# A window-ratio kernel on one core: in every second duo of batch 1, one pair of rows takes its denominator from shifted adds on POOL and DVE and a single matmul

## The reference: what is computed

```python
def _L0_conv_ref(x):                                   # WINDOW = (1, 5, 20), FILL = 1.0
    s = box_sum(box_sum(x, 1, w0), 2, w1)
    num = box_sum(s * s, 3, w2)
    d = box_sum(box_sum(box_sum(x * x, 1, w0), 2, w1), 3, w2)
    c0 = box_sum(jnp.ones((x.shape[1],), x.dtype), 0, w0)
    c1 = box_sum(jnp.ones((x.shape[2],), x.dtype), 0, w1)
    norm = c0[:, None] * c1[None, :]
    return jnp.nan_to_num(num / (d * norm[None, :, :, None]), nan=FILL)
x = x + _L0_conv_ref(_gn(x))                           # _gn: group norm, 32 groups of 6 channels
```

## Time and profile before

| | |
|---|---|
| device time, median of 3 runs | 402.33 us (401.9 to 404.88) |
| device time of the profiled execution | 402.03 us |
| its span | 400.3 us |
| PE busy | 373.6 us (93%) |
| DVE busy | 262.8 us (66%) |
| ACT busy | 276.7 us (69%) |
| POOL busy | 233.6 us (58%) |
| mean granted TensorE clock | 0.984 of full speed |

### The profile page before, as it was taken

How to read it: one execution, slowest core, us unless ns; L and a number is a source line. 1 busy time by engine, 2 the same in 40 slices (tenths; PEclk the granted TensorE clock), 3 DMA queues, 4 the chain that set the end, 5 groups by cost and what they waited for, 6 DMA issues and landing times.

```text
span 400.3 us, 8088 instructions
## 1 busy us (share of the span) xinstructions
PE 373.6 (93%) x3156; PEld 372.2 (93%) x3156; DVE 262.8 (66%) x552; ACT 276.7 (69%) x368; POOL 233.6 (58%) x150
## 2 busy tenths in 40 slices
PE   1999989999999999996789999999999999999983
PEld 1999979999999999996789999999999999999982
DVE  2999942676779999999755544555545554455545
ACT  1465539989999999976146776667766677666751
POOL 4000054888888888884156676666766667666431
PEclk9999999999999999999689999999999999999998
DMA  8999100589999852242002222222112222222213
GB/s 244 327 327 328 38 0 2 158 250 285 279 288 285 271 160 80 93 130 90 6 2 79 80 81 80 79 80 74 45 43 78 79 80 80 80 79 80 70 44 124
DMA packets 66485, 50.84 MB, mean 127 GB/s; under 512 B 912, under 2 KB 66448, under 8 KB 66448
## 3 DMA queue, kind: packets, MB, share of 16 engines
q1 hardware_dynamic: 66448, 50.34, 40.7%
HBM read 25.17 MB, written 25.17 MB: 126 GB/s over the span
## 4 chain that ended last, share of the span: by engine, by line
PE 81%; DVE 9%; ACT 4%; issue 2%; DMA 2%; POOL 1%; DVEq 0%; POOLq 0%; ACTq 0%
PE N L443 21%; PE U L434 18%; PE D L443 16%; PE S L434 16%; PE N L434 5%; PE S L443 4%; DVE late_triples L576 4%; DMA xs<-x 2%; DVE ratio L640 2%; DVE N L643 2%; DVE ratio L649 1%; ACT xs L374 1%; POOL xc L309 1%; ACT q L392 1%; ACT q L398 1%
## 5 line engine op out<-in xcount | busy, mean ns | idle before, releaser
L315 POOL TENSOR_TENSOR xs<-xs,ratio 128x768 f32<-128x768 f32 x63 | 114.4, 1817 | 98.4 <-DVE ratio L649 98.4
L309 POOL TENSOR_TENSOR xc<-xs,mean_c 128x768 f32<-128x768 f32 x64 | 117.0, 1830 | 60.1 <-DVE mean_c L585 48.1
L640 DVE SCALAR_TENSOR_TENSOR ratio<-D,q 128x768 f32<-128x768 f32 x51 | 48.7, 954 | 93.9 <-ACT q L398 93.9
L643 DVE SCALAR_TENSOR_TENSOR N<-N,q 128x768 f32<-128x768 f32 x64 | 61.6, 962 | 10.0 <-PE N L443 6.2
L649 DVE SCALAR_TENSOR_TENSOR ratio<-ratio,N 128x768 f32<-128x768 f32 x64 | 61.1, 954 | 6.8 <-DVE N L643 0.5
L365 ACT ACTIVATE xs<-S 128x768 f32<-128x768 f32 x36 | 29.2, 811 | 51.5 <-PE S L434 51.5
L392 ACT ACTIVATE q<-D 128x768 f32<-128x768 f32 x51 | 41.3, 810 | 30.7 <-PE D L443 30.7
L398 ACT ACTIVATE q<-q 128x768 f32<-128x768 f32 x64 | 54.0, 844 | 2.0
L434 PE MATMUL S<-b,xc 128*128 128x128 f32 x432 | 55.1, 278 | 0.0
L443 PE MATMUL N<-b_r,xs 128*128 128x138 f32 (+2 forms) x384 | 54.3, 292 | 0.0
L434 PE MATMUL U<-b5d,xs 128*128 128x128 f32 x432 | 54.0, 275 | 0.0
(11 more groups left out here) (64 smaller groups left out, 383.9 us busy)
## 6 DMA issues: line engine op xcount, KB each, us to landing
out<-xs SPq DMA_DIRECT2D x31, 768.0 KB, 3.8
xs<-x SPq DMA_DIRECT2D x8, 1536.0 KB, 14.8
xs<-x SPq DMA_DIRECT2D x16, 768.0 KB, 5.5
out<-xs SPq DMA_DIRECT2D x2, 384.0 KB, 2.9
```

The lines of the kernel that those rows point to most:

```text
L309: nc.gpsimd.tensor_tensor(pairs(xc[:, n % XC_RING, :]), pairs(x_flat(n)), mean, ALU.subtract)\
L315: nc.gpsimd.tensor_tensor(x_flat(n), x_flat(n), ratio[:, n % RATIO_RING, :], ALU.add)\
L640: nc.vector.scalar_tensor_tensor(t1, in_bank(d_bank(n)), -TINY, pairs(q[:, n % Q_RING, :]), ALU.add, ALU.mult).then_inc(t1_ready, 1)
L643: nc.vector.scalar_tensor_tensor(in_bank(N), in_bank(N), TINY, pairs(q[:, n % Q_RING, :]), ALU.add, ALU.mult).then_inc(t2_ready, 1)
```

## The change

In 16 of the 32 duos of batch 1 (33, 35, ... 63) the second pair's D is made in the other order: first along the channels, by adds, and then along W, by a matmul that needs no transposed data.

- POOL multiplies the pair's xc2 by the inverse variance spread over channels and writes it between two margins of ten zeros (`sum_twos`: 2 x 192 elements), and adds it to itself shifted by one (2 x 211). It does this in its step n before finish(n), for duo n+3.
- DVE adds the result to itself shifted by 2, 4 and 8 (`sum_sixteens`, three adds with a wait between them, ahead of t1(n), for duo n+1), and adds the sums of 16 and of 4 after t1(n) (`sum_twenties`).
- PE makes 3 matmuls in place of 6 for U and for D of that duo, and one more, `D[:, 1, 0:384] <- b5d x of_20` with 384 moving columns, that waits for `of_20_ready`. ACT copies one pair of U in place of two.
- Once: two small memsets on POOL ahead of centre(32), a matmul for the group variance in duo 29, and on DVE in duo 29 four instructions that spread its inverse over channels.

```diff
+        def summed(n):
+            return FIRST_SUMMED <= n < TOTAL and (n - FIRST_SUMMED) % SUMMED_EVERY == 0
...
+            def sum_twos(n):
...
+                nc.gpsimd.tensor_tensor(scaled[:, :, MARGIN:MARGIN + C], pair, inv_var_c, ALU.mult)\
+                  .then_inc(scaled_ready, 1)
+                pool.wait_ge(scaled_ready, k + 1)
+                nc.gpsimd.tensor_tensor(of_2[:, :, 0:PADDED - 1], scaled[:, :, 0:PADDED - 1], scaled[:, :, 1:PADDED],
+                                        ALU.add).then_inc(of_2_ready, 1)
...
                     pool.wait_ge(mean_ready, 2)
+                    clear_margins()
                 if m < TOTAL:
                     centre(m)
+                if summed(n + SQUARE_AHEAD):
+                    sum_twos(n + SQUARE_AHEAD)
                 finish(n)
...
-                box20(d_bank(n), u[:, n % U_RING, :], batch(n)).then_inc(d_ready, 1)
+                mm = box20(d_bank(n), u[:, n % U_RING, :], batch(n), own_pairs(n))
+                if summed(n):
+                    pe.wait_ge(of_20_ready, (n - FIRST_SUMMED) // SUMMED_EVERY + 1)
+                    mm = nc.tensor.matmul(D[:, 1, 0:PCOLS], b5d[:, :], of_20, start=True, stop=True)
+                mm.then_inc(d_ready, 1)
...
+            def sum_sixteens(n):
+
+                dve.wait_ge(of_2_ready, (n - FIRST_SUMMED) // SUMMED_EVERY + 1)
+                shifted_sum(of_4, of_2, of_2, 2, PADDED - 3).then_inc(of_4_ready, 1)
+                dve.wait_ge(of_4_ready, (n - FIRST_SUMMED) // SUMMED_EVERY + 1)
+                link(shifted_sum(of_8, of_4, of_4, 4, PADDED - 7))
+                link(shifted_sum(of_16, of_8, of_8, 8, C))
+
+            def sum_twenties(n):
...
+                shifted_sum(of_20.rearrange("p (r c) -> p r c", r=PAIR), of_16, of_4, C_WIN - 4, C)\
+                  .then_inc(of_20_ready, 1)
...
             def quotient(n, before_ratio=None):
 
+                if summed(n + 1):
+                    sum_sixteens(n + 1)
                 dve.wait_ge(q_ready, n + 1)
...
                                                ALU.add, ALU.mult).then_inc(t1_ready, 1)
+                if summed(n + 1):
+                    sum_twenties(n + 1)
                 dve.wait_ge(n_ready, n + 1)
```

More of the change, by code:

```diff
@@ L47 @@
 XC2_SLOT, S2_SLOT, LATE_SLOTS = HALF, HALF + 2, 2
+SUM_SLOT, INV_SLOT = HALF + 4, RAW + HALF
+FIRST_SUMMED, SUMMED_EVERY = DUOS + 1, 2
+MARGIN = C_LO
+PADDED = C + 2 * MARGIN
 LOADS = 8
@@ L118, in window_ratio_kernel @@
         offsets_ps = S[:, 1, PCOLS:PCOLS + CHUNKS * COEFS]
+        sums = xs[:, SUM_SLOT * STEP:(SUM_SLOT + 2) * STEP, :].rearrange("p r c -> p (r c)")
+        taken = PAIR * PADDED
+        scaled, of_2, of_4, of_8, of_16 = [
+            sums[:, i * taken:(i + 1) * taken].rearrange("p (r c) -> p r c", r=PAIR) for i in range(5)]
+        of_20 = sums[:, 5 * taken:5 * taken + PCOLS]
+        inv_var_c = xs[:, INV_SLOT * STEP:INV_SLOT * STEP + PAIR, :]
+        group_var_ps = stats_ps[1][:, GROUPS + CHUNKS:2 * GROUPS + CHUNKS]
         loaded0 = [sem(f"loaded0_{j}") for j in range(LOADS)]
@@ L140, in window_ratio_kernel @@
         inv_ready = sem("inv_ready")
+        inv_c_ready = sem("inv_c_ready")
+        scaled_ready = sem("scaled_ready")
+        of_2_ready = sem("of_2_ready")
+        of_4_ready = sem("of_4_ready")
+        of_20_ready = sem("of_20_ready")
         xc_ready = sem("xc_ready")
@@ L179, in slot, with own_pairs @@
             return t if t < HALF else RAW + t - HALF
+        def summed(n):
+            return FIRST_SUMMED <= n < TOTAL and (n - FIRST_SUMMED) % SUMMED_EVERY == 0
+        def own_pairs(n):
+            return 1 if summed(n) else DUO
         def x_rows(n, duos=1):
@@ L316, in finish, with clear_margins @@
                   .then_inc(out_ready, 1)
+            def sum_twos(n):
+                k = (n - FIRST_SUMMED) // SUMMED_EVERY
+                pool.wait_ge(xc2_ready, n + 1)
+                if k == 0:
+                    pool.wait_ge(inv_c_ready, 1)
+                else:
+                    pool.wait_ge(of_4_ready, k)
+                pair = xc2_of(n)[:, PCOLS:2 * PCOLS].rearrange("p (r c) -> p r c", r=PAIR)
+                nc.gpsimd.tensor_tensor(scaled[:, :, MARGIN:MARGIN + C], pair, inv_var_c, ALU.mult)\
[3 more added lines that the diff above has]
+                                        ALU.add).then_inc(of_2_ready, 1)
+            def clear_margins():
+                pool.wait_ge(n_ready, RAW_DUOS)
+                nc.gpsimd.memset(scaled[:, :, 0:MARGIN], 0.0).then_inc(pool_own, 1)
+                nc.gpsimd.memset(scaled[:, :, MARGIN + C:PADDED], 0.0).then_inc(pool_own, 1)
+                pool.wait_ge(pool_own, own[0] + 2)
             for j in range(LOADS):
@@ L355, in keep_u @@
                     act.wait_ge(d_ready, n - U_RING + 1)
-                nc.scalar.activation(pairs(u[:, n % U_RING, :]), in_bank(U), ACT.Copy).then_inc(us_ready, 1)
+                own = own_pairs(n)
+                nc.scalar.activation(pairs(u[:, n % U_RING, :])[:, 0:own, :], in_bank(U)[:, 0:own, :], ACT.Copy)\
+                  .then_inc(us_ready, 1)
             def square_s(n):
@@ L427, in _, with box5 @@
         def _(pe):
-            def box5(bank, rows, weights):
-                for i in range(DUO):
+            def box5(bank, rows, weights, own=DUO):
+                for i in range(own):
                     for j in range(CHUNKS):
@@ L436, in box5, with box20 @@
                 return mm
-            def box20(bank, data, b):
-                for i in range(DUO):
+            def box20(bank, data, b, own=DUO):
+                for i in range(own):
                     for j, (first, end) in enumerate(SPAN):
@@ L469, in box_u @@
                     pe.wait_ge(us_ready, n)
-                box5(U, xc2_of(n), b5d).then_inc(u_ready, 1)
+                box5(U, xc2_of(n), b5d, own_pairs(n)).then_inc(u_ready, 1)
             def sum_d(n):
@@ L513, in average_squares @@
                                           averager[0][:, 0:1], start=True, stop=True)
+                if b:
+                    mm = nc.tensor.matmul(group_var_ps, averager[0][:, :],
+                                          ssq_c[:, 0, :].rearrange("p (g c) -> p g c", g=GROUPS)[:, :, 0],
+                                          start=True, stop=True)
                 return mm
@@ L612, in scale_late_bands @@
             def scale_late_bands():
+                spread_late_inverse()
                 link(fold_variance(1))
@@ L618, in scale_late_bands, with spread_late_inverse, shifted_sum @@
                 ins.then_inc(b20_ready, 1)
+            def spread_late_inverse():
+                inv_g = mean_sum[:, :]
+                link(nc.vector.tensor_scalar(inv_g, group_var_ps, 1.0 / COUNT[0], EPS, ALU.mult, ALU.add))
+                link(nc.vector.reciprocal(inv_g, inv_g))
+                t = INV_SLOT - RAW
+                dve.wait_ge(stored[t % 2], 16 * (t // 2 + 1))
+                for r in range(PAIR):
+                    ins = nc.vector.tensor_copy(inv_var_c[:, r, :].rearrange("p (g c) -> p g c", g=GROUPS),
+                                                inv_g.unsqueeze(2).to_broadcast([128, GROUPS, GC]))
+                ins.then_inc(inv_c_ready, 1)
+            def shifted_sum(to, a, b, shift, cols):
+                return nc.vector.tensor_tensor(to[:, :, 0:cols], a[:, :, 0:cols], b[:, :, shift:shift + cols], ALU.add)
+            def sum_sixteens(n):
[5 more added lines that the diff above has]
+            def sum_twenties(n):
+                k = (n - FIRST_SUMMED) // SUMMED_EVERY
+                if k:
+                    dve.wait_ge(d_ready, n - SUMMED_EVERY + 1)
+                shifted_sum(of_20.rearrange("p (r c) -> p r c", r=PAIR), of_16, of_4, C_WIN - 4, C)\
+                  .then_inc(of_20_ready, 1)
             def keep_offsets():
```

## The result

| | before | changed |
|---|---|---|
| device time, median | 402.12 us (401.9 to 404.88, 4 runs) | 415.4 us (414.45 to 419.68, 4 runs) |
| ratio, 95% interval | | 1.0335 (1.0248 to 1.0422) |
| two duos of batch 1, by the trace | 11.14 us | 12.11 us |

A forecast was written before the change was run, and what follows sets the result against it. PE was taken to bound the kernel at 11.14 us for two duos; with DVE and POOL excluding each other, 14 x 1.58 = 22.1 us lost, less 0.4 once and 0.7 credit, gave 423 us from 402.0, range 405 to 444.

The forecast's parts named there:

- Exclusion, taking turns: Batch 1: DVE adds with two SBUF inputs and POOL operations exclude each other, longest waiter next; 423 us, chance 0.63.
- The length of the train: Two duos with the shifted adds in batch 1: 12.72 us against 11.14, 1.58 us lost each time.
- a credit of 0.15 us: POOL-to-DVE handovers: DVE starts 0.15 us before POOL's recorded end; three take 0.45 off, giving 12.27 us.
- the walk: Step-by-step sum through two duos of batch 1, DVE and POOL taking turns, from first add to next: 12.72 us.
- the end: Kernel's end: PE's D(63) waits for t1(62), and the fourth add standing between t1 and t2 makes it 0.6 late.
- The feared tipping: In a train, POOL's next finish goes ahead of the first add: 13.71 us for two duos, some 13.2 with credit.
- PE's part: Each summed duo loses 1.395 us of U and D and gains a 0.64 us matmul: 0.75 saved, 12 in all.
- POOL's part: POOL's two new operations per summed duo, multiply and shifted add: 0.96 and 1.05 us, 2.01 together.
- The transition: Transition to batch 1: margins delay centre(32), so L594 comes first and takes 0.3 instead of 1.92; 1.3 us back.
- No exclusion: Rival: L594 was slow for another reason, so adds run freely beside POOL and nothing waits; 391 us, chance 0.15.
- POOL always first: Rival: DVE gets in only when POOL waits for a semaphore; two duos 14.83 us, total 453 us, chance 0.14.
- the hidden exclusion: Rival: handovers overlap and waits fall in POOL's idle time; two duos about 11.1 us, 398 to 406, chance 0.08.

The follow-up runs named there:

- the run with one input: Changed kernel with each shifted DVE add replaced by a same-size reduction reading one SBUF tensor, sums wrong: 389.6 us, ratio 0.9666.
- the ceiling: Changed kernel with all sums on POOL and DVE left out and of_20 filled once with ones: 390.08 us, ratio 0.9698.
- POOL's sums alone: Changed kernel with DVE's four adds left out, POOL's multiply and shifted add kept, of_20 filled once: 393.73 us, ratio 0.9699.
- PE undone: Changed kernel with all sums made but unused, PE making U and D of both pairs as before the change: 420.28 us, ratio 1.0445.
- the first add early (first run): Changed kernel with the first shifted add (of_4) moved one duo earlier, ahead of the previous duo's t1, nothing left out: 395.06 us, ratio 0.9797.

## Why the prediction was right, point by point

**Exclusion, taking turns: right.** The forecast took one row, L594's 1920 ns, for a DVE instruction with two SBUF inputs standing still beside POOL. The run with one input decides it: the same adds fall to 0.54 to 0.58 us and two duos to 10.39. It was 423 us forecast and 415.4 measured, inside the range.

**The length of the train: 12.72 forecast, 12.11 measured.** The mis-sized term is the handover. I had a credit of 0.15 us for POOL to DVE, counted three of them, and then took back nearly all. The trace has it in both directions: the second add ends 0.46 us after the finish's recorded end and needs 0.59, and the finish ends 1.68 us after the first add's and needs 1.82. Four handovers of some 0.14 lie between the first add and t1, which takes 306.46 to 311.31, 4.85 us, and not the 5.40 of the walk. The 0.55 is all but 0.06 of the difference. The rule of the Trainium skill ("SBUF — State Buffer", section "Who interferes with whom"), that the loser blocks fully, is borne out by the adds' 2.09 us, except for these 0.14 us at each end.

The two profiled executions differ by 17.7 us in span, and the trace divides it so: 2.9 us before the mean of batch 1 is spread (the clock), 0.2 less at the transition, 14 x 0.97 = 13.6 for the trains, and 1.4 at the end, from the t1 of duo 59 on (29.6 us against 28.2). I had put the end at 0.6. Some 0.9 of the 1.4 is a low clock, 0.76 from 405 to 412 us, after PE had idled 2.19 us: there D(63) takes 1.24 and 1.29 us for its two parts, which take 0.96 and 0.66 in a train. That the medians differ by 13.3, almost the trains alone, is in part luck: the end costs something, and the transition can give something back (below).

**The feared tipping did not come.** POOL's next finish waits for the same ratio that frees DVE, and DVE's queue goes on 0.17 us earlier (306.46 and 306.63), so the first add gets in first (589 ns as the mean of 12 trains).

**What closes the train: wrong, without effect on the sum.** The walk let POOL's finish and centre (3.65 us) set the next first add. It is DVE's own queue behind the next duo's q. From the t1 at 311.31 to the next first add at 318.58 it is 7.27 us by that path, and 7.32 by the walk. The two are near each other by chance. For the same reason PE's wait is not for of_20 (about 2 us, I wrote) but 1.1 us for t1, one step earlier; by the time that PE has made the first half of D, of_20 is there. PE needs 10.39 of the 12.11 us, so 1.7 are lost to it in two duos; by the window from 310 to 340 us it idles 3.74 of 30, which is 1.5 in two duos, where I wrote 2.3.

**PE's part: right.** The matmul with 384 columns adds 0.66 us in the chain (0.64 taken), and the ceiling is 390.08 us (12 us saved forecast).

**POOL's part: a little high.** Undisturbed, in the kernel with POOL's sums alone, the multiply takes 1.01 and the shifted add 0.89 us, 1.90 for 2.01.

**The transition: wrong.** I counted 1.3 us back because L594 would be free. It was, but the next pair with two SBUF inputs was blocked in its place, a row that I had not walked on to. PE's wait fell only from 1.36 to 1.12 us, and the clock fell behind it as before (0.50 from 206 to 208 us). From one D to the next the stretch takes 9.46 us (200.48 to 209.94) against 9.47 before (197.81 to 207.28), so nothing came back. The part that I had left to the range, the clock, can come back: in the kernels with POOL's sums alone, with PE undone and with the first add early (first run), whose instructions are the same up to there, PE waited 0.97 to 1.02 us, the clock stayed at 1.00 and the stretch took 7.67 to 7.72 us, 1.8 less. Whether it does so in the faster executions of the changed kernel is not shown, since only the slowest was traced. With POOL waiting for that pair as well the stretch takes 6.46.

**The rivals.** No exclusion (391 us) is what the run with one input gives, 389.6. POOL always first (453) and the hidden exclusion (398 to 406) did not occur.

## What to carry to other kernels

Before work is moved to DVE and POOL, list for each DVE instruction whether both inputs lie in SBUF. For those, add DVE's and POOL's times, and not each by itself. Where they cannot be avoided, put each one where POOL waits for something anyway, one at a time: two in a chain behind a POOL operation that is ready cost a whole POOL operation each, and here moving a single add by one duo was worth 20 us. A single odd row (one instruction six times its price) is worth following up, on to the next instruction of the same kind.

## What the runs showed of the hardware

- A DVE instruction with two SBUF inputs and a POOL operation that reads SBUF (centre, finish and both new ones do) overlap by about 0.14 us in their records at a handover, in both directions, and otherwise not at all; one with one SBUF input, or with one SBUF and one PSUM input, is not slowed (542 to 584 ns, 954 ns).
- The two take turns while both have work: POOL's finish and centre, the second ready as the first ended, did not run back to back while an add was waiting (finish, add, centre, add from 306.63 to 311.29 us, and the means over 12 trains agree). That the turn goes to the one that has waited longer fits, and so does plain alternation; nothing here tells them apart.
- POOL's add of a tile to itself shifted by one, 422 elements, takes 0.89 us, and its multiply of two tiles of 384 takes 1.00 to 1.01.
- The granted clock between 50 and 70 us, ahead of anything that was changed, differs from one execution to the next: 1.00 in seven of the eleven traces, 0.74 in one and 0.66 in three. The matmul over `mean_sum` starts at 192.5 to 193.4 us in the seven, at 195.8 in the one and at 198.7 to 198.9 in the three, so this moves the time by 3 to 6 us. That is likely most of the scatter in these runs (of the changed kernel's four, the slowest has a mean clock of 0.967, the two fastest 0.987 and 0.991), and the reason why rhythms settle more than medians here.
- At the transition the clock fell to 0.50 for some 2 us after PE had waited 1.12, 1.32 or 1.36 us (the changed kernel, the one without sums, the one before), and stayed at 1.00 after waits of 0.62 to 1.02 us (four executions). From one D to the next that is 9.46 to 9.67 us against 7.32 to 7.72, the waits included. What decides it is not shown.
